# The edge network of a graph layer, two batches in step on the four quarters of the matrix array

## The reference, cut to what matters

```python
h = edge_feats                                  # (20000, 8)
for W in (W_mlp1, W_mlp2, W_mlp3):              # 8x64, 64x64, 64x64
    h = SILU_2MOM * jax.nn.silu(h @ W / jnp.sqrt(jnp.float32(W.shape[0])))
```

## Time and profile before

| | us |
|---|---|
| median of 3 runs (1967.13 to 1970.70) | 1968.84 |
| the profiled execution, its own time | 1976.71 |
| its span in the trace | 1975.1 |
| from the first step of the edge network to the first instruction of the next block | 848.9 to 959.6 |

### The profile page before, as it was taken

How to read it: one execution, slowest core, us unless ns; L and a number is a source line. 1 busy time by engine, 2 the same in 40 slices (tenths; PEclk the granted TensorE clock), 3 DMA queues, 4 the chain that set the end, 5 groups by cost and what they waited for, 6 DMA issues and landing times. The chain is left out here.

```text
span 1975.1 us, 33502 instructions
## 1 busy us (share of the span) xinstructions
PE 1664.8 (84%) x9860; PEld 1172.0 (59%) x9861; DVE 989.9 (50%) x1998; ACT 697.0 (35%) x1609; POOL 558.2 (28%) x637
## 2 busy tenths in 40 slices
PE   1991067789999978779799999957999999898994
PEld 0540012258888855555599999955555555654663
DVE  8320245556766747735100000046999999742233
ACT  0220022235555532344321122115555555441331
POOL 6777400010110002215100000023555555224133
PEclk6996555579999999979899999975999999998997
DMA  6200280011101032054656556035555555528986
GB/s 171 59 7 6 68 323 0 0 22 22 22 11 21 1 93 60 0 204 138 238 213 247 192 215 241 18 102 162 174 154 154 149 165 153 157 93 250 361 265 188
DMA packets 131140, 252.81 MB, mean 128 GB/s; under 512 B 35345, under 2 KB 52597, under 8 KB 126573
## 3 DMA queue, kind: packets, MB, share of 16 engines
q1 hardware_dynamic: 91692, 171.81, 26.1%
q0 software_dynamic: 39360, 79.86, 14.3%
HBM read 196.03 MB, written 55.52 MB: 127 GB/s over the span
## 5 line engine op out<-in xcount | busy, mean ns | idle before, releaser
L1999 PE MATMUL acc<-prod,ohy 128*64 128x256 f32 x1056 | 248.7, 386 | 5.8 <-DVE prod L2114 5.8
L2043 ACT ACTIVATE ohy<-oh,RECS 128x64 f32<-128x64 f32 x704 | 187.0, 336 | 150.5 <-PE acc L1999 150.5
L678 PE MATMUL ps<-ohS,ohD 128*128 128x512 f16 x352 | 122.6, 453 | 129.8 <-DVE ohS L660 115.9
L1999 PEld LDWEIGHTS acc<-prod,ohy 128*64 128x64 f32 x1056 | 138.4, 137 | 130.9 <-issue 69.5
L1976 POOL DMA_INDIRECT rows<-up_dram,idx x176 | 167.0, 949 | 143.6 <-DVE prod L2114 101.2
L267 POOL DMA_INDIRECT rec_dram<-recs,pos x157 | 160.5, 1022 | 60.3 <-issue 48.9
L2002 PE MATMUL acc<-prod,ohy 128*64 128x256 f32 x704 | 177.4, 395 | 0.0
L1766 DVE TENSOR_SCALAR FT<-y_ps,b2T 128x188 f32<-128x188 f32 x32 | 13.2, 414 | 319.2 <-PE y_ps L1715 319.2
L1703 PE MATMUL hid_ps<-FT,W 128*128 128x188 f32 x1024 | 168.2, 326 | 0.7 <-ACT FT L1740 0.7
L2114 DVE TENSOR_TENSOR prod<-w_ps,rows 128x768 f32<-128x768 f32 x176 | 166.7, 947 | 0.0
L1703 PEld LDWEIGHTS hid_ps<-FT,W 128*128 128x128 f32 x1024 | 165.8, 193 | 0.9 <-issue 0.9
(11 more groups left out here) (381 smaller groups left out, 2675.3 us busy)
## 6 DMA issues: line engine op xcount, KB each, us to landing
W<-in_L_ffn_w SPq DMA_DIRECT2D x16, 4096.0 KB, 15.8
bankW_sp<-in_L_ffn_W_sp SPq DMA_DIRECT2D x2, 4096.0 KB, 24.6
xin<-zeros SPq DMA_DIRECT2D x31, 256.0 KB
h_dram<-h3e SPq DMA_DIRECT2D x22, 256.0 KB, 4.5
h<-h_dram SPq DMA_DIRECT2D x22, 256.0 KB, 2.7
QF<-q_dram SPq DMA_DIRECT2D x20, 250.0 KB, 4.0
xin_sp<-zeros SPq DMA_DIRECT2D x17, 256.0 KB
xin_fq<-zeros SPq DMA_DIRECT2D x17, 256.0 KB
```

Of the source, the lines that this page charges most:

```text
L678: last = nc.tensor.matmul(ps[:, bass.ds(region + c0, cn)], ohD[:, slot, :], ohS[:, slot, c0:c0 + cn], start=False, stop=False, skip_group_ ...
L1999: upper = lambda m: nc.tensor.matmul(acc[0:HALFB, bank, :].rearrange("p (b c) -> p b c", c=MUL)[:, m:4:3 - m, :], ohs[:, 1 + m, :], pr[:, ...
L2043: last = nc.scalar.activation(ohy[:, t % OHY, i, :], oh[:, par, t, :], ACT.Copy, scale=RECS[:, bass.ds(BATCH * g + t, 1), 4 + i])
```

## The change

The two batches of a pair go through the stages in step. There are now 11 pairs and 4 steps for each, 44 in all; one step of PE works on both batches and writes both banks, and it waits for ACT's copies of both. ACT copies bank 0, then bank 1. In place of one product on the whole array with block diagonal weights, stages 1 to 3 issue four products on the four quarters: 64 rows of weights (`halves[q]`) and 64 columns of output (`halves[c]`). Row half q writes bank q, so a bank now holds half of each batch, and what was a batch's half changes place from stage to stage; the store puts it back in the old order, with two pieces of 1 KB per partition for each transfer. The block diagonal weights are loaded as before, and only their diagonal blocks are read. The number of transposes, silus, stored bytes and their sizes stay.

The hand-written order counts in the new steps: 4 first, 8 before the small products, then one step after an even round and two after an odd one, and 2 at the end.

```diff
-                if 4 * r + stage > 0:
-                    pe.wait_ge(out[x], 4 * r + stage)
+                else:
+                    for bank in range(2):
+                        pe.wait_ge(out[bank], step)
...
                 elif stage == 1:
-                    for j in range(cols // 128):
-                        used = REC * cols // 64
-                        last = nc.tensor.matmul(banks[x][:, 128 * j:128 * (j + 1)], W[0][0:used, j, :], fT[0:used, x, :],
-                                                start=True, stop=True)
+                    for i in range(4):
+                        x, group = divmod(i, 2)
+                        for q in range(2):
+                            for c in range(2):
+                                last[q] = nc.tensor.matmul(banks[q][halves[c], 128 * i:128 * (i + 1)],
+                                                           W[0][halves[q], 2 * q + group, halves[c]], fT[halves[q], x, :],
+                                                           start=True, stop=True)
                 else:
                     src = (h1, h2)[stage - 2]
-                    last = nc.tensor.matmul(banks[x][:, 0:cols], W[stage - 1][:], src[:, x, 0:cols], start=True, stop=True)
-                last.then_inc(done[x], 1)
+                    for c in range(2):
+                        for q in range(2):
+                            last[q] = nc.tensor.matmul(banks[q][halves[c], :], W[stage - 1][halves[q], halves[q]],
+                                                       src[halves[q], c, :], start=True, stop=True)
+                for bank in range(2):
+                    last[bank].then_inc(done[bank], 1)
...
+                for bank in range(2):
+                    act.wait_ge(done[bank], step + 1)
+                    if stage == 0:
+                        nc.scalar.activation(fT[:, bank, :], banks[bank][:, 0:128], ACT.Copy).then_inc(out[bank], 1)
+                        continue
+                    kept = (2 * r + bank) % 4
+                    if stage == 3 and r >= 2:
+                        act.wait_ge(stored[kept], 16 * (r // 2))
+                    dst = (h1[:, bank, :], h2[:, bank, :], h3[:, kept, :])[stage - 1]
+                    nc.scalar.activation(dst, banks[bank][:], ACT.Silu, scale=scales[stage - 1]).then_inc(out[bank], 1)
...
-                LAYERS = 8 * -(-ECHUNKS // 2)
-                FIRST, SECOND = 8, 24
+                LAYERS = 4 * EPAIRS
+                FIRST, SECOND = 4, 12
...
-                            for step in range(SECOND + 3 * n, SECOND + 3 * (n + 1)):
+                            for step in range(SECOND + 3 * n // 2, SECOND + 3 * (n + 1) // 2):
                                 layer_pe(pe, step)
-                        for step in range(SECOND + 6 * TILES, LAYERS):
+                        for step in range(SECOND + 3 * TILES, LAYERS):
                             layer_pe(pe, step)
```

More of the change, by code:

```diff
@@ L38 @@
 ECHUNKS = -(-ETILES // 8)
+EPAIRS = ETILES // 16
+assert EPAIRS * 16 == ETILES
 REC = 16
@@ L1301, in edge_layers @@
             scales = (1 / math.sqrt(8), SILU_2MOM / math.sqrt(EHID), SILU_2MOM / math.sqrt(EHID))
[L1303 to L1309, removed]
+            halves = (slice(0, EHID), slice(EHID, 2 * EHID))
             def on_pe(pe, step):
-                r, stage, x, batch, cols = where(step)
-                if batch >= ECHUNKS:
+                r, stage = divmod(step, 4)
+                if r >= EPAIRS:
                     return
@@ L1316, in on_pe @@
                     pe.wait_ge(loaded, all_loaded)
-                if 4 * r + stage > 0:
-                    pe.wait_ge(out[x], 4 * r + stage)
+                else:
+                    for bank in range(2):
+                        pe.wait_ge(out[bank], step)
+                last = {}
                 if stage == 0:
-                    tiles = cols // 64
-                    last = nc.tensor.transpose(banks[x][0:REC * tiles, 0:128],
-                                               RECS[:, 8 * batch:8 * batch + tiles, :].rearrange("p t w -> p (t w)"), ident[:])
+                    for x in range(2):
+                        first = 8 * (2 * r + x)
+                        last[x] = nc.tensor.transpose(banks[x][:, 0:128],
+                                                      RECS[:, first:first + 8, :].rearrange("p t w -> p (t w)"), ident[:])
@@ L1352, in all_stored, with store @@
+            def store(sp, r):
+                for bank in range(2):
+                    kept = (2 * r + bank) % 4
+                    sp.wait_ge(out[bank], 4 * r + 4)
+                    sp.dma_start(h3_dram[:, 1024 * r:1024 * (r + 1)].rearrange("p (x w) -> p x w", x=2)[:, :, 256 * bank:256 * (bank + 1)],
+                                 h3[:, kept, :].rearrange("p (x w) -> p x w", x=2)).then_inc(stored[kept], 16)
             def all_stored(sp):
-                for b in range(4):
-                    sp.wait_ge(stored[b], 16 * len(range(b, ECHUNKS, 4)))
+                for kept in range(4):
+                    sp.wait_ge(stored[kept], 16 * len(range(kept // 2, EPAIRS, 2)))
@@ L1389, in _ @@
                         sync_work(sp)
-                        for b in range(ECHUNKS):
-                            store_hidden(sp, b)
+                        for r in range(EPAIRS):
+                            store_hidden(sp, r)
                         all_stored(sp)
```

## The result

The changed kernel takes **2001.51 us** (median of 4 runs, 2000.7 to 2002.99). The kernel before, run beside it, has a median of 1969.46 us (4 runs, 1967.13 to 1970.7): ratio 1.0165, 95% interval 1.0147 to 1.0183. It is slower by 1.65%. The forecast was 2001 us. The profiled execution took 2000.7 us, with a span of 1999.1 us; the one before took 1976.71 us for a span of 1975.1 us. So the medians differ by 32 us and the two profiled executions by 24 us; the last part of this text comes back to that.

The account below looks back on a forecast made before the run. The prediction took PE, nearly always busy in the placing of the first expert layer, as the bound. Terms priced at 1.2 GHz throughout sum to +32.3 us on the median 1968.84: 2001 us, 8-in-10 range 1973 to 2012.

Parts of the forecast that it names:

- transposes of the choices: Two sets of ten transposes ahead of the copies and one behind take twice as long at half clock: +3.1 us.
- two pairs: The two pairs of batches ahead of the rounds: 21.1 us at 1.2 GHz against 15.4, +5.7 us.
- rounds: The 19 rounds with comparisons, at 3/8 of an 11.3 us pair each: 80.5 us against 63.3, +17.2 us.
- tail to the last silu: From the last comparison to the last silu's end: 11.9 us against 7.2, +4.7 us.
- behind the last silu: The stretch where the last transfers land and engines meet: stays 9.2 us, the store's smaller pieces costing nothing to +0.5.
- Four quarters at once: In the layers' products, four quarter products run concurrently, so a layer of a pair streams 0.85 us instead of 1.71.
- Two at once: Rival for the layers' products: only two quarters run concurrently, 1.71 us a layer at full clock; 1990 to 1993 us, chance 0.17.
- one at a time: Rival for the layers' products: no concurrency, 1.7 us more on each of 33 layers; over 2040 us, chance 0.03.
- A wait for both banks: In each step PE and ACT take turns: a full step is 2.25 us at 2.4 GHz, 3.15 at 1.2.
- The clock stays at 0.50: TensorE's clock in the placing stays at 1.2 GHz throughout, since the array streams less: +32.3 us in all, chance 0.43.
- it goes to and fro: Rival: the clock alternates between half and full in the rounds; +18 or +8 us, 1977 to 1987 us, chance 0.18.
- The store lands in the same 9.2 us: Behind the last silu: the store follows the tail, scatters are no longer last, and the stretch stays 9.2 us.

## Why the prediction was right, and where its sum was not

Against the profiled execution of before, term by term:

| term | predicted | measured in the profiles |
|---|---|---|
| first pair | +0.5 | 9.5 - 8.7 = +0.8 |
| transposes of the choices | +3.1 | 7.7 - 5.7 = +2.0 |
| two pairs | +5.7 | 21.2 - 15.4 = +5.8 |
| ten small products | +1.1 | 2.1 - 1.2 = +0.9 |
| rounds | +17.2 | 80.2 - 63.3 = +16.9 |
| tail to the last silu | +4.7 | 12.1 - 7.2 = +4.9 |
| behind the last silu | +0 | 3.1 - 9.2 = -6.1 |
| sum | +32.3 | +25.2 |

- **Four quarters at once**: right (1.98 us for eight passes, 1.09 at full clock). Two at once and one at a time fall.
- **A wait for both banks**: right. A step was priced at 3.15 us at 1.2 GHz and 2.25 at 2.4, and took 3.26 and 2.35.
- **The rounds**: 80.2 us against the 80.5 of the sum is closer than the working was. It took 19 x 3/8 = 7.125 pairs, but in the new order 19 rounds hold 28 steps, which is 7 pairs: 1.4 us less at the priced 11.3 us. A pair took 80.2 / 7 = 11.5. The two errors nearly cancel. The shares of streaming that the prediction gives for 1.2 GHz, 54% and about 72%, come to 53% and 74% by its own terms; nothing changes with that.
- **The clock stays at 0.50**: right. That the low clock is what costs with the quarters is shown: with dummy products (same quarters, same wait) it is 1.00 and the time is about that of the kernel before. With the zeros back it is 1.00 as well. That it goes to and fro falls for this kernel; it is what the kernels with dummies in the rounds do (0.89 and 0.90). The kernel with dummies ahead alone fell from 1.00 to 0.50 between 882 and 886, as it entered its rounds, with PE busy for 69.32 of 79.30 us and no pause above 1.28 us in them. The Trainium skill, "TensorE: Matmul & The Clock Gate", section "Why this matters for your kernels", ties the fall to idle gaps longer than any in these rounds. The trace disagrees with it, as it did in the prediction. Why the clock falls stays open: both ways of getting it back shortened PE's pauses and put more work on the whole array, and no run changed one of these alone.
- **Transposes of the choices**: 1.1 us too much. The clock rose for some us there (0.72 in that stretch), while I had it low throughout.
- **The store lands in the same 9.2 us**: wrong, and by far the largest error of the sum, 6.1 us. The prediction said that the scatters are no longer last, and that the stretch stays. Both can't be: in the kernel before the scatters *were* what ended it, as the kernel without the last of them shows. In the timeline of the two kernels, the last scatter's issue stands like this, first before, then after:

```profile
949.84 1.18 POOL L1415 DMA_INDIRECT xin<-N,slot_in  x1 [0.31 <-issue]
```

```profile
978.13 1.18 POOL L1424 DMA_INDIRECT xin<-N,slot_in  x1 [0.30 <-issue]
```

The last silu ends at 950.36 in the one and at 983.03 in the other, so the scatter was issued 0.5 us ahead of that end in the first and 4.9 us in the second. Slowing the tail paid part of its own price.

**The nearness of 2001 to 2001.51 is in part luck.** In the profiles the placing grew by 25.2 us, it began 1.3 us later, what follows it took 2.5 us less, and the span grew by 24.0 us. By a sum of 26 the forecast would have been 1995 us. The prediction also put the profiled execution at about 2009 us; it took 2000.7. The medians differ by 32 us because the profiled execution of before was 7.3 us above its median and that of after 0.8 below its own; the rounds of the former were 3.1 us longer, by the low clock, than those of another execution. Where the other 4 us of it lie stays open. In the three later comparisons the kernel before had medians of 1974.15, 1973.72 and 1976.37 us, so the 32 us themselves are uncertain by some 5.

## What to carry to other kernels

Before zeros are taken out of a product, ask what keeps TensorE's clock: here half of the streaming went, and the clock went with it; giving the clock back took 31 to 36 us off. The better gain was not in the products at all: look at the wait behind a stage, find the transfer that ends it, and move independent work behind its issue, not ahead of it. A sum that moves one engine's end has to ask again what else ended the stretch.

## What the runs showed of the hardware

- Added work can shorten a kernel: one or two 256-column dummy products in most pauses took 31 to 36 us off.
- PE's busy share does not tell its clock: 90% busy at 1.00 and 88% busy at 0.50 in the same stretch of two kernels.
- Halving the streaming on the array bought nothing at the half clock: the eight passes of a layer end in 1.98 us, while the four whole-array passes of both batches end in 1.96 us at full clock, and the rounds with the zeros ran 14.7 us faster (65.5 against 80.2).
- The same instructions, from the first comparison to that of round 17, took 50.1 us in one execution at full clock and 55.3 in another with low spells.
- The last store of h3 landed 5.7 us after its issue in the kernel before, beside the last scatters, and 2.1 us after it in the kernel without them.
